# Parking twenty instead of ten turned tiles of chunk 0 in a four-layer graph kernel

## What is computed

```
x = _layernorm(x + U @ (scale[:, None] * (Vt @ (x @ weight))) + bias)      # U = Vt = adj
x = _layernorm(x + relu((inv_deg[:, None] * A_prime @ x) @ W.T + b))       # A_prime = a*adj, diagonal + (1-a)
z = leaky_relu(_lap_mul(adj, x) @ W1 + b1)
S = exp(-distances(z) / 2), of each row only the k = 4 largest             # A2 = S + adj
x = _layernorm(x + _lap_mul(A2, x) @ W2 + b2)
x = _layernorm(x + relu(concat([x, adj @ x]) @ W.T + b))
```

## Time and profile before

| | |
|---|---|
| runs | 1411.88, 1412.84, 1417.01 us; median 1412.84 |
| profiled execution | 1415.97 us, span of its instructions 1414.3 us |
| TensorE busy | 1385.4 us, 98% of the span |
| VectorE, ScalarE, GpSimd busy | 842.8, 457.6, 239.5 us |
| DMA | 407.53 MB, mean 288 GB/s |
| L697, copy to the high part | 190 staged or parked in the region, mean 595 ns |
| L1113, split to the low part | 190 likewise, mean 687 ns |
| stores L518 | 38 of 768 KB and 38 of 512 KB |
| parked stores L521 | 2 of 1,280 KB, 9.1 us to landing |

### The profile page before, as it was taken

One profiled execution on the slowest core, in us unless ns is written; L12 is line 12 of the kernel. 1 busy time (PEld: TensorE's weight loads), 2 busy tenths in 40 slices (PEclk: granted clock), 3 DMA queues, 4 the chain that ended last, 5 costly groups with the idle time before them and its releaser, 6 DMA issues.

```text
span 1414.3 us, 19936 instructions
## 1 busy us (share of the span) xinstructions
PE 1385.4 (98%) x7369; PEld 795.8 (56%) x7369; DVE 842.8 (60%) x1306; ACT 457.6 (32%) x967; POOL 239.5 (17%) x362
## 2 busy tenths in 40 slices
PE   7999999999999999999999999999999999999998
PEld 6888887777544445544444545444444444444467
DVE  6877776666323423434323259999999946655144
ACT  6766665555300000000000126655555410000011
POOL 1111111110100100000000000111111167777000
PEclk9999999999999999999999999999999999999999
DMA  9999989887999879997787803303444699999973
GB/s 326 383 381 390 361 325 348 338 301 269 340 390 354 346 301 390 411 359 296 299 320 273 324 19 98 104 16 119 134 135 134 220 390 405 403 372 400 386 252 116
DMA packets 111410, 407.53 MB, mean 288 GB/s; under 512 B 11664, under 2 KB 28048, under 8 KB 89568
## 3 DMA queue, kind: packets, MB, share of 16 engines
q1 hardware_dynamic: 79520, 316.43, 60.0%
q0 software_dynamic: 19440, 73.71, 13.3%
q10 hardware_dynamic: 12368, 16.26, 3.2%
HBM read 339.77 MB, written 66.58 MB: 287 GB/s over the span
## 4 chain that ended last, share of the span: by engine, by line
PE 75%; DVE 17%; DMA 5%; ACT 1%; issue 1%; SPq 0%; DVEq 0%
PE acc L1291 10%; PE acc L1293 10%; PE acc L1292 10%; DVE hT L1176 8%; PE pt L1361 6%; PE pt L1291 5%; PE pt L1293 5%; PE pt L1292 5%; DVE wT L1177 4%; DMA region<-in_adj 4%; DVE wz_sb L1177 3%; PE acc L1341 3%; PE acc L1345 3%; PE acc L1343 3%; PE pnat L1258 2%; PE pxT L1332 1%
## 5 line engine op out<-in xcount | busy, mean ns | idle before, releaser
L1361 PE MATMUL pt<-ident,region 128*128 128x128 f32 x1024 | 242.6, 278 | 14.4 <-DMA region<-in_adj 14.2
L1361 PEld LDWEIGHTS pt<-ident,region 128*128 128x128 f32 x1024 | 200.4, 196 | 40.1 <-issue 9.0
L1291 PE MATMUL acc<-region,yop 128*128 128x512 f16 (+1 forms) x581 | 217.8, 375 | 0.4 <-DMA region<-at_scratch 0.4
L1293 PE MATMUL acc<-region,yop 128*128 128x512 f16 (+1 forms) x581 | 217.5, 374 | 0.0
L1292 PE MATMUL acc<-region,yop 128*128 128x512 f16 (+1 forms) x581 | 217.5, 374 | 0.0
L1113 DVE SCALAR_TENSOR_TENSOR region<-pt,region 128x512 f16<-128x512 f32 x190 | 129.2, 687 | 71.7 <-ACT region L697 71.4
L747 ACT ACTIVATE region<-pt 128x512 f32<-128x512 f32 x256 | 133.0, 603 | 112.0 <-PE pt L1457 46.5
L697 ACT ACTIVATE region<-pt 128x512 f16<-128x512 f32 x190 | 112.2, 595 | 99.6 <-PE pt L1361 91.6
L1176 DVE MAX8 hT<-region 128x8 f32<-128x4096 f32 x31 | 136.6, 4406 | 1.3 <-ACT region L747 1.3
L1450 PE MATMUL pt<-yop 128*128 128x512 f16 x256 | 98.0, 383 | 5.8 <-ACT region L747 4.2
L654 ACT ACTIVATE std<-mv,eps_ln 128x4 f32<-128x4 f32 x31 | 9.2, 297 | 284.6 <-DVE mv L920 284.6
(11 more groups left out here) (261 smaller groups left out, 2301.9 us busy)
## 6 DMA issues: line engine op xcount, KB each, us to landing
region<-at_scratch SPq DMA_DIRECT2D x163, 1280.0 KB, 8.2
region<-in_adj SPq DMA_DIRECT2D x128, 512.0 KB, 8.0
at_scratch<-region POOLq DMA_DIRECT2D x38, 768.0 KB, 7.0
at_scratch<-region POOLq DMA_DIRECT2D x38, 512.0 KB, 7.1
region<-at_scratch SPq DMA_DIRECT2D x76, 256.0 KB, 2.7
x_scratch<-xout ACTq DMA_DIRECT2D x16, 256.0 KB, 11.1
region<-at_scratch ACTq DMA_DIRECT2D x3, 1280.0 KB, 9.7
gath_all<-x_scratch POOLq DMA_DIRECT2D x12, 256.0 KB, 5.2
```

Source lines behind the costliest of these rows:

```text
L1291: nc.tensor.matmul(into, y[:, 0, kt, :], high, start=(kt == first_tile), stop=False)
L1293: return nc.tensor.matmul(into, y[:, 1, kt, :], high, start=False, stop=(kt == last_tile))
L1361: ins = nc.tensor.transpose(pt[kt % 4][:, t * P:(t + 1) * P], nat[u % 4][:, t, b * BLOCK + j:(b + 1) * BLOCK:PAIR], ident[:, :])
```

## The change

`PARKED_UNITS` becomes 4 and `PARKED` 5: units 0 to 3 of chunk 0, tiles 7 to 26, wait in `kept` from chunk 5's first tile on, over the parts of chunks 5, 6 and 7. They are stored behind units (4, 0), (4, 2), (5, 1) and (6, 1). Instead of one wait of ScalarE at the first tile of chunk 6 for both stores, there are three, at the first tiles of chunks 5, 6 and 7, for 2, 3 and 4 stores. The other edits correct the counts of staged units, of which chunk 0 now has one.

```diff
-PARKED = 6
-PARKED_UNITS = 2
-PARKED_AT = {(5, 0): 0, (5, 2): 1}
+PARKED = 5
+PARKED_UNITS = 4
+PARKED_AT = {(4, 0): 0, (4, 2): 1, (5, 1): 2, (6, 1): 3}
+PARKED_BEFORE = {5: 2, 6: 3, 7: 4}
...
-                    units = NCH * UPC // 2 - 1 if u >= UPC - 2 + s else (UPC + 1 - s) // 2 - 1
-                    for part in range(len(STORES)):
+                    units = NCH * UPC // 2 - PARKED_UNITS // 2 if u >= UPC - 2 + s else (UPC + 1 - s) // 2 - PARKED_UNITS // 2
+                    for part in range(len(STORES) if units > 0 else 0):
...
-                    if kt == 0 and c == PARKED:
-                        act.wait_ge(parked_stored, 16 * PARKED_UNITS)
+                    if kt == 0 and c in PARKED_BEFORE:
+                        act.wait_ge(parked_stored, 16 * PARKED_BEFORE[c])
...
-                        if (kt - KEPT) % UNIT == 0 and c * UPC + u >= 4:
+                        if (kt - KEPT) % UNIT == 0 and c * UPC + u >= PARKED_UNITS + 2:
...
-                            if (kt - KEPT) % UNIT == k0 and c * UPC + u >= 4:
-                                act.wait_ge(stage_stored[s][part], 16 * ((c * UPC + u) // 2 - 1))
+                            if (kt - KEPT) % UNIT == k0 and c * UPC + u >= PARKED_UNITS + 2:
+                                act.wait_ge(stage_stored[s][part], 16 * ((c * UPC + u) // 2 - PARKED_UNITS // 2))
```

## The result

The change makes the kernel slower by 0.42%. Over nine runs each its median is 1420.46 us against 1415.33 of the kernel before; the ratio is 1.0042, interval 1.0031 to 1.0053. I had taken 0.5% as the least that could be told from no change; the interval tells 0.42%. I had forecast 1411.8 and a range from 1407 to 1416.5, and slower only as a rival. The forecast started from the three runs known then, with a median of 1412.84; over nine the kernel before stands 2.5 us higher, and that much of the miss is not the change's.

A forecast was written before the change was run, and what follows sets the result against it. In the transposing pass TensorE is almost never idle, losing some 9 us to late loads. Terms -0.2 + 4.0 - 4.9 = -1.1 us took the 1412.84 us median to 1411.8, range 1407 to 1416.5.

The forecast's parts named there:

- The store at (4, 2): Start of chunk 5: TensorE newly waits 2.7 to 3.1 us for loads, perhaps with half clock; 4.0 us lost.
- the loads' loss in ten us: After a parked store, the loads' queue moves 1.32 MB instead of 1.92: 0.60 MB less, 3.1 us at 192 GB/s.
- the delay of those stores: Staged stores of units 3 and 4 go up to 6.4 us later; ScalarE's refill cost 0, at worst 1 us.
- The clock: Start of chunk 5: if the clock falls after the wait as at 264.86, 1.7 us come on top.
- the new stall is longer: Rival, chance 0.17: chunk 5's start loses 8.0 us, from both chunk 4 stores or ScalarE's wait; 1415.7 us in all.
- The 4.9 us gained at chunk 6: Start of chunk 6: with (5, 1) for (5, 2), wait and half clock go; 4.9 us gained, bounds 3.4 and 4.9.
- Chunk 0's saving: Chunk 0: four fewer staged stores, 2.62 MB, little carried to chunk 2; 0.2 us gained, bounds 0 and 1.0.
- The rival that it is carried on: Chance 0.05: chunk 0's saving also removes the 4.1 us lost in chunks 2 to 4; -9.0 us, 1404.
- The store at (4, 0): Chunk 4, at about 185: the DMA has room for 2.4 MB against 1.31 MB; cost 0.
- ScalarE's waits for parked stores: First tiles of chunks 5, 6 and 7: cost 0; at chunk 5, 1 to 2 us without the load wait's cover.
- The stores at (5, 1) and (6, 1): Chunks 5 and 6, at about 239 and 292: the DMA has room, or the chunk loses nothing now; no cost.
- The sentence on taking turns: DMA engines alternate queues by packet: beside 10,240-byte parked rows, loads would lose 0.47 MB or 2.4 us; wait 2.0.

The follow-up runs named there:

- the pair of kernels with late stores: Parked stores moved to (6, 0) and later, timing only: the change with four units, 0.9988 of the kernel before; the kernel before with two units, 0.9989.
- four units stored late: The change with its four parked stores moved behind (6, 0), (6, 1), (6, 2) and (7, 0), timing only: 1411.39 us, 0.9988 of the kernel before.
- the version with (4, 1): The change with unit 1's parked store moved from (4, 2) to (4, 1): 1415.90 us, 1.0024 of the kernel before.
- the none-parked kernel: The change with no tile parked, chunk 0 staging its 25 tiles as every other chunk does: 1415.02 us, 1.0005 of the kernel before.

## Why the prediction was wrong

**The store at (4, 2), taken at 4.0 us.** This is the step that failed. The place and the kind were right: TensorE waits for the loads of chunk 5, with the clock at half behind it, and (4, 2) makes it, not (4, 0). The size was 9.2 us, in two profiles. Three parts of the working were too small, or held only for the place that they were read from:
- I took the loads' loss in ten us, 0.60 MB, and let it end there. After the change the loads get 0.66 MB less in the first ten us and 0.59 less in the next ten, against 1.92 and 1.93. At the 192 GB/s of the prediction the 1.25 MB are 6.5 us, where I had 3.1; the waits are 5.4 us in one profile and 6.3 in the other. GpSimd's staged stores of units 3 and 4 stand behind the parked one and go on pressing (the first of them lands after 11.3 us, before after 8.3). As I read it now, the loads' 1.92 MB in the earlier trace rows was not their share between two full queues; it was what the stores left over. I had the delay of those stores in the text, and priced it only for ScalarE.
- I had read the loss from chunk 6, where the DMA had run below its full rate until 248 and only unit 1 came late. There the loads were back at 1.88 MB in the second ten us, from 258 to 268, so ending the loss after ten us was right for that place. In chunk 4 the DMA is full from 200 on, and GpSimd has more to store: its queue moved 5.44 MB in the 20 us behind the parked store, and 4.76 in the 20 us from 248.
- The clock, taken at 1.7 us once, cost 3.4 (twice 1.7) in one profile and 2.6 in the other.

The rival "the new stall is longer" had 8.0 us at this place and a chance of 0.17; it named the store at (4, 0), together with the next, or ScalarE's wait as its cause. ScalarE's wait was not it, and (4, 0) has only the 1.4 us. That the rival's 8.0 is near the 9.2 is luck.

**The 4.9 us gained at chunk 6.** The mechanism was right, (5, 2) to (5, 1) takes the wait away each time. The size came from one execution. In two others the same place lost 0.7 and 1.5 us, so the mean of three is 2.3, and the runs value the clean start at 0.13% (1.8 us, with an interval that takes in zero). With these profiles I would have put about 2 here.

**The other terms.** Chunk 0's saving, taken at 0.2 with a bound of 1.0: nothing that shows, by the pair of kernels with late stores. The rival that it is carried on and takes away the whole 4.1 us of chunks 2 to 4 is refuted; a gain below 1 us is not. The store at (4, 0), taken at 0: about 1.4 us, and 1.5 where it stands alone in chunk 4. ScalarE's waits for parked stores: nothing in the change, as taken. The stores at (5, 1) and (6, 1): nothing, as taken.

**The sum again.** Losses by interval are 12.1 us in the mean of two profiles of the change and 6.6 in the mean of three of the kernel before: 5.5 us more. The runs say 0.42% of 1415.33, 5.9 us, or 5.1 by the medians. My sum had 4.0 - 4.9 - 0.2. Of the difference, 5.2 us are the loss at chunk 5 (9.2 for 4.0) and 2.6 the gain at chunk 6 (2.3 for 4.9). Against them, the first three intervals lose 1.3 us less in the change's two profiles than in the three of before; with four units stored late they do not (3.8), so this is not shown to come from the change.

**The sentence on taking turns.** The trace shows 1.52 MB for 1.26 in the first ten us and little over 20 (2.69 for 2.60). So the rule points the right way, and for the parked store's rows alone it explains the smaller part. Whether it also sets the share beside the staged stores, whose rows are two and three times a load's, no run here shows.

**What stays open.** Which waits cost the clock was seen and not tried: in these profiles no fall follows single waits up to 1.80 us; one comes with each of 2.44 us or more, and with the pair of 1.96 and 1.82 in the version with (4, 1). Why the loads get about a third when GpSimd has much queued was not tried apart; a kernel with the staged stores in rows of 2,048 bytes would tell. What else spreads the runs of one kernel is open too: the version with (4, 1), which starts chunk 6 clean, goes from 1413.7 to 1419.9 us.

## What to carry to other kernels

A transfer that is moved out of a crowded stretch is worth only what the engine at the bound waited for there, and here that was nothing for the second ten tiles. Where it is put, all of it can come out of the loads: here 1.25 of 1.31 MB, within 20 us, in a stretch with the DMA full and a load with 0.4 us of lead. Put such stores where the trace shows the DMA below its full rate and the next loads are well ahead; of the versions here two units stored at (4, 0) and (5, 0), or at (5, 0) and (5, 1), are the fastest that compute the whole (0.9985 and 0.9987 of the kernel before). They cannot be told apart, and only the interval of the first leaves out 1. Before a wait is priced, look at a second profile: the same wait was 0.40, 1.19 and 3.05 us.

## What was new about the hardware

With much queued on GpSimd's side, the loads' queue moves 1.2 to 1.5 MB in ten us and the stores' 2.5 to 2.9, with the parked store in rows of 10,240 bytes as in rows of 2,048 (the staged stores beside it have 6,144 and 4,096). After the first load of the program, the fourteen profiles have seven waits of TensorE of 2.44 us or more in pass 0, and half clock (0.50 granted) comes with each. By the interval, or for the none-parked kernel by the stretch at 0.50 (33 to 36 us), it adds some 1.7 us for the four of 2.44 to 3.05 us, and 2.6 to 2.8 for the three of 3.53, 4.89 and 6.30.
